# Paired maxima and exponents, and a new step table for the next batch's preparation, in a gated cross-attention and mixture-of-experts kernel

## The reference

```python
xn = layer_norm(ctx, gamma_x, beta_x)            # [8, 375, 256], the context
ln = layer_norm(layernorm(x), gamma_l, beta_l)   # [8, 112, 256], the latents
q = (ln @ Wq) * 64 ** -0.5                       # 8 heads of 64
k_x, v_x = split(xn @ Wkv); k_x = rope(k_x)      # 375 keys, rotated
k_l, v_l = split(ln @ Wkv)                       # 112 keys
attn = softmax(q @ concat(k_x, k_l).T)           # 112 x 487 for each head
x = x + tanh(g0) * (attn @ concat(v_x, v_l)) @ Wo
...
P = softmax(layernorm(x) @ Wg); P_norm = the two largest of P, normalized
x = x + tanh(g1) * sum_e P_norm[e] * (gelu(layernorm(x) @ W1[e] + b1[e]) @ W2[e] + b2[e])
```

## Time and profile before

| | |
|---|---|
| time, median of 3 runs | 532.35 us (531.82 to 533.09) |
| the profiled execution | 532.01 us, span 530.3 us |
| TensorE busy | 442.8 us, 84% of the span |
| VectorE busy | 303.9 us, 57% |
| ScalarE busy | 268.4 us, 51% |
| GpSimd busy | 192.1 us, 36% |
| mean granted TensorE clock | 0.919 of full speed |
| scores of batch 0 to scores of batch 7 | 72.75 to 283.47 us |

### The profile page before, as it was taken

How to read it: one execution, slowest core, us unless ns; L and a number is a source line. 1 busy time by engine, 2 the same in 40 slices (tenths; PEclk the granted TensorE clock), 3 DMA queues, 4 the chain that set the end, 5 groups by cost and what they waited for, 6 DMA issues and landing times. The chain is left out here.

```text
span 530.3 us, 9193 instructions
## 1 busy us (share of the span) xinstructions
PE 442.8 (84%) x3173; PEld 372.4 (70%) x3173; DVE 303.9 (57%) x715; ACT 268.4 (51%) x568; POOL 192.1 (36%) x211
## 2 busy tenths in 40 slices
PE   1689868897989979798888773589999999999990
PEld 1578646575756757575665662369999999999990
DVE  4564632436263453626354733548888888888850
ACT  2322245645646574564646611037676766776630
POOL 4231027272544627264460147301332222233322
PEclk9999969897999999799999965559999999999997
DMA  7200000000001009950008012576777778884323
GB/s 218 84 1 29 0 22 9 5 27 1 30 1 30 0 27 286 237 139 0 1 5 314 1 45 64 198 226 222 209 200 208 203 220 227 240 252 81 47 29 89
DMA packets 41863, 56.04 MB, mean 106 GB/s; under 512 B 1745, under 2 KB 37153, under 8 KB 41808
## 3 DMA queue, kind: packets, MB, share of 16 engines
q1 hardware_dynamic: 36864, 49.80, 30.8%
q0 software_dynamic: 4960, 5.72, 6.9%
HBM read 40.37 MB, written 16.07 MB: 106 GB/s over the span
## 5 line engine op out<-in xcount | busy, mean ns | idle before, releaser
L1356 POOL DMA_INDIRECT acc_scratch<-yv,xt x28 | 49.0, 1752 | 130.7 <-DVE yv L1509 126.5
L1378 ACT ACTIVATE hf<-ph,b1t 128x256 f32<-128x256 f32 x112 | 47.1, 472 | 48.3 <-PE ph L1584 47.7
L851 DVE TENSOR_REDUCE negmax<-sc 112x1 f32<-112x487 f32 x64 | 42.2, 660 | 37.2 <-PE sc L1092 37.2
L1092 PE MATMUL sc<-keys,queries 64*112 64x488 f32 x128 | 37.9, 671 | 24.0 <-ACT prob L649 22.3
L649 ACT ACTIVATE prob<-sc,negmax 112x487 f32<-112x487 f32 x64 | 43.0, 672 | 21.3 <-DVE negmax L851 21.3
L1117 PEld LDWEIGHTS po<-probt,vals 125*64 125x64 f32 (+1 forms) x512 | 27.5, 148 | 25.6 <-issue 16.3
L1100 PE MATMUL pt<-ident,prob 112*125 112x112 f32 x256 | 41.3, 286 | 3.4 <-ACT prob L649 3.4
L1100 PEld LDWEIGHTS pt<-ident,prob 112*125 112x125 f32 x256 | 37.0, 198 | 8.9 <-ACT prob L649 5.2
L1491 DVE TENSOR_TENSOR hl<-hf,hh 128x512 fp32r<-128x512 f32 x56 | 38.8, 693 | 1.9
L1489 DVE CAST hh<-hf 128x512 fp32r<-128x512 f32 x56 | 24.1, 431 | 23.8 <-ACT hf L1378 23.2
L657 ACT COPY probt<-pt 125x448 f32<-125x448 f32 x64 | 34.5, 540 | 5.0 <-PE pt L1100 4.9
(11 more groups left out here) (303 smaller groups left out, 1321.7 us busy)
## 6 DMA issues: line engine op xcount, KB each, us to landing
w_first<-in_L_ffn_W SPq DMA_DIRECT2D x10, 1024.0 KB, 8.4
w_next<-in_L_ffn_W SPq DMA_DIRECT2D x10, 1024.0 KB
rows_scratch<-blank SPq DMA_DIRECT2D x2, 4257.0 KB, 32.5
w_third<-in_L_ffn_W SPq DMA_DIRECT2D x8, 1024.0 KB, 8.0
xt<-rows_scratch SPq DMA_DIRECT2D x14, 258.0 KB, 2.8
ctx_t<-in_ctx SPq DMA_DIRECT2D x8, 375.0 KB
w_first<-in_L_xattn_Wkv SPq DMA_DIRECT2D x1, 1024.0 KB, 9.0
x_all<-in_x SPq DMA_DIRECT2D x2, 448.0 KB, 5.2
```

Of the source, the lines that this page charges most:

```text
L851: dve.tensor_reduce(negmax[:, h % 2:h % 2 + 1], sc[h % 2][0:M, 0:JA], AX, ALU.max, negate=True).then_inc(max_done.sem, 1)
L1092: pe.matmul(sc[u][0:M, 0:JP], queries[r, p, a], keys[r, p, a], start=True, stop=True, tile_position=(u * DH, 0)).then_inc(score_done.sem, 1)
L1356: pool.indirect_dma_start(out=acc_dram, out_offset=bass.IndirectOffsetOnAxis(ap=xt[i % 3][:, n, D + 1:D + 2].bitcast(I32), axis=0), in_=yv ...
L1378: last = act.activation(hf[:, n % 3, u], ph[n % 3][:, u * T:(u + 1) * T], ACT.Gelu, bias=b1t[:, col])
```

## The change

There are five parts.

1. Order in the pairs. VectorE does the maxima of heads h+2 and h+3 together in an even head h, and the two reciprocals (`invert`) together in an odd one. ScalarE does `keep_prob` first in a head, and both exponents, h+2 and h+3, in the even head h. Before, each head did one of each.
2. The table of steps. LEAD goes from 8 to 10, AHEAD (how many steps the second batch stands behind the first in the opening) from 13 to 15, and most steps have new numbers. SPLIT_AT is (2, 4, 6, 8) and OUTPUT_AT (9, 10, 12).
3. The copy of x1row into x_all goes from VectorE to POOL (`keep_x1`, behind the power of the output's norm), and the next x1row waits for it.
4. The opening: the low part of Wq is subtracted on VectorE, not POOL, the second norm of the latents stands ahead of the first split, and the latents' keys and values fall in other steps.
5. The second half of x is loaded ahead of the weights, and the four gamma and beta vectors by ScalarE's queue.

The core of the diff:

```diff
-        LEAD = 8
-        AHEAD = 13
+        LEAD = 10
+        AHEAD = 15
         VALUES_AT = (2, 4, 6, 8)
-        SPLIT_AT = (3, 4, 7, 8)
+        SPLIT_AT = (2, 4, 6, 8)
         PROJECT_AT = (9,)
-        OUTPUT_AT = (9, 10, 13)
+        OUTPUT_AT = (9, 10, 12)
...
# POOL, prepare
-                if s == 9:
+                if s == 10:
                     if not first:
                         rotate(pool, t, p, 0)
-                if s == 11:
+                if s == 13:
                     if not first:
                         rotate(pool, t, p, 1)
-                if s == 13:
+                if s == 16:
                     if not first:
                         rotate(pool, t, p, 2)
...
+            def keep_x1(t, p):
+                pool.wait_ge(x1_done.sem, x1_done.at(t, p, 1))
+                pool.tensor_copy(x_all[:, bass.ds(2 * t + p, 1), :].rearrange("q a d -> q (a d)"), x1row[:]) \
+                    .then_inc(x1_kept.sem, 1)
             def late_rstd(t, p, h, previous):
                 for n, batch in due(OUTPUT_AT[1:2], h, (t, p), previous):
                     output_rstd(*batch)
+                    keep_x1(*batch)
...
# ScalarE, head
+                keep_prob(t, p, h)
                 prepare_beside(prepare, h, 0, following, after)
-                keep_prob(t, p, h)
+                if h % 2 == 0:
+                    if h + 2 < H:
+                        exponent(t, p, h + 2)
+                        exponent(t, p, h + 3)
+                    elif following:
+                        exponent(*following, 0)
+                        exponent(*following, 1)
                 prepare_beside(prepare, h, 1, following, after)
                 late_high_out(t, p, h, previous)
-                if h + 2 < H:
-                    exponent(t, p, h + 2)
-                elif following:
-                    exponent(*following, h + 2 - H)
...
# VectorE, opening
+            latent_norm(1)
             split_latents(0)
-            latent_norm(1)
+            dve.wait_ge(whi_done, 1)
+            dve.tensor_tensor(deep[1][:, 0:4, :], w2s[:, 0:4, :], deep[0][:, 0:4, :].bitcast(F32),
+                              ALU.subtract).then_inc(wql_done, 1)
             split_latents(1)
...
# VectorE, output
+                    dve.wait_ge(x1_kept.sem, x1_kept.at(t, p, 0))
...
-                    dve.tensor_copy(x_all[:, row, :].rearrange("q a d -> q (a d)"), x1row[:])
...
# VectorE, head
-                if h + 1 < H:
-                    invert(t, p, h + 1)
-                elif following:
-                    invert(*following, 0)
+                if h % 2 == 0:
+                    if h + 2 < H:
+                        row_max(t, p, h + 2)
+                        row_max(t, p, h + 3)
+                    elif following:
+                        row_max(*following, 0)
+                        row_max(*following, 1)
                 prepare_beside(prepare, h, 0, following, after)
-                if h + 2 < H:
-                    row_max(t, p, h + 2)
-                elif following:
-                    row_max(*following, h + 2 - H)
                 prepare_beside(prepare, h, 1, following, after)
+                if h % 2:
+                    if h + 1 < H:
+                        invert(t, p, h + 1)
+                        invert(t, p, h + 2)
...
# TensorE, prepare: one line of the table
-                if s == 7:
+                if s == 8:
                     project_keys(t, p, 0)
```

More of the change, by code:

```diff
@@ L339, in frame @@
         def frame(eng, prepare, latents, begin, head, close):
-            for s in range(AHEAD + LEAD - 2):
+            for s in range(AHEAD + LEAD - 3):
                 prepare(0, 0, s, first=True)
@@ L345, in frame @@
             begin(0, 0)
-            for s in range(LEAD - 2, LEAD):
+            for s in range(LEAD - 3, LEAD):
                 prepare(0, 1, s)
@@ L387, in _ @@
             load_latents(0)
-            for n, v in enumerate((gamma_x, beta_x, gamma_l, beta_l)):
-                sp.dma_start(affine_rows[n * KD:(n + 1) * KD, :], v.rearrange("(k p) -> k p", p=P)) \
-                    .then_inc(affine_loaded, 16)
+            load_latents(1)
             sp.dma_start(w2s[:, 0:4, :].rearrange("p (k a) d -> p k (a d)", k=KD),
@@ L419, in _ @@
         def _(pool):
-            for c in (crstd_done, cl_done, rope_done, krow_done, orstd_done, row_copied):
+            for c in (crstd_done, cl_done, rope_done, krow_done, orstd_done, row_copied, x1_kept):
                 c.start(pool)
@@ L572, in latents @@
                     act.activation(gates[:], gates[:], ACT.Tanh).then_inc(tanh_done, 1)
+            for n, v in enumerate((gamma_x, beta_x, gamma_l, beta_l)):
+                act.dma_start(affine_rows[n * KD:(n + 1) * KD, :], v.rearrange("(k p) -> k p", p=P)) \
+                    .then_inc(affine_loaded, 16)
             act.wait_ge(wq_loaded, 16)
@@ L626, in prepare @@
                     split_context(t, p, 1)
-                if s == 8:
+                if s == 9:
                     raw_key(t, p, 0)
-                if s == 9:
+                if s == 11:
                     keep_value(t, p, 0)
-                if s == 10:
+                if s == 12:
                     raw_key(t, p, 1)
-                if s == 11:
+                if s == 14:
+                    keep_key(t, p, 0)
+                if s == 16:
+                    raw_key(t, p, 2)
+                if s == 17:
                     keep_value(t, p, 1)
-                if s == 12:
-                    raw_key(t, p, 2)
-                if s == 13:
-                    keep_key(t, p, 0)
+                if s == 19:
+                    keep_key(t, p, 1)
+                if s == 20:
                     keep_value(t, p, 2)
-                if s == 16:
-                    keep_key(t, p, 1)
-                if s == 18:
+                if s == 21:
                     keep_key(t, p, 2)
@@ L836, in prepare @@
                                           crstd[:, j:j + 1], ALU.subtract, ALU.mult).then_inc(cnorm_done.sem, 1)
-                if s == 9:
+                if s == 10:
                     if first:
                         rotate(dve, t, p, 0)
-                if s == 11:
+                if s == 12 and not first:
+                    copy_latents(t, p)
+                if s == 13:
                     if first:
                         rotate(dve, t, p, 1)
-                if s == 13:
+                if s == 16:
                     if first:
                         rotate(dve, t, p, 2)
-                if s == 14 and not first:
-                    copy_latents(t, p)
             def row_max(t, p, h):
@@ L865, in begin @@
                 invert(t, p, 0)
+                invert(t, p, 1)
             def output(t, p, part):
@@ L1065, in prepare @@
                     transpose_context(t, p, 1)
[L1066 removed]
+                if s == 8:
                     project_keys(t, p, 0)
[L1068 removed]
+                if s == 9:
                     project_values(t, p, 0)
[L1070 removed]
+                if s == 11:
                     project_keys(t, p, 1)
[L1072 removed]
+                if s == 13:
+                    transpose_keys(t, p, 0)
+                if s == 14:
+                    project_keys(t, p, 2)
+                if s == 15:
                     project_values(t, p, 1)
[L1074 to L1077 removed]
+                if s == 17:
+                    transpose_keys(t, p, 1)
+                if s == 18:
                     project_values(t, p, 2)
[L1079 to L1081 removed]
+                if s == 20:
                     transpose_keys(t, p, 2)
```

52 lines of the change are left out of this document (20 added, 32 removed).

## The result

The changed kernel takes 560.46 us (median of 4 runs, 557.13 to 561.60); the kernel before took 532.72 us on the same chip (4 runs, 531.82 to 535.26). The ratio is 1.050, 95% interval 1.044 to 1.056: slower by 5%, and outside the forecast range of 526 to 550. The profiled execution took 560.93 us, its span 559.2.

The account below looks back on a forecast made before the run. TensorE was taken as the bound (25.39 of 30.20 us busy). Five batches +13.3, opening -1.2, first batch -2.7, batch 6 +1.7, last stretch -1.5 sum to +9.6 on 532.01: 541.5 us, range 536 to 547, 8 of 10 526 to 550.

Parts of the forecast that it names:

- Stall 2.55: Each batch: TensorE's key transposes wait 2.55 us for POOL's third rotation, which starts behind the output norm's power and x1row copy.
- Stall 2.4: Each batch: the next context's transposes wait 2.4 us for VectorE's normalization, its small statistics operations held beside POOL's rotation.
- Stall 2.0: Each batch: the output projection waits 2.0 us for VectorE's heads, since out_t stands behind an exponent on ScalarE.
- Stall 1.2: Each batch: the next context's first projection waits 1.2 us for POOL's low part, behind ScalarE's exponent and five copies.
- I take the lost clock to stay hidden here: Five batches: no time added for TensorE's lower clock, since half-clock work behind the context's transposes runs into the next stall.
- rival B: TensorE's lost clock has a price, towards the upper end of the range; chance 0.15.
- From the last batch's scores on ... -1.5, bounds -5 and +2: Last batch's scores to the end: pairs save waits, the rotations' work is gone, ten POOL scatters stay; -1.5 us.
- it takes 25.1: First batch: 21.7 us of full-clock work, a key stall of 1.0 and a context stall of 2.4; -2.7 us against 27.86.
- Opening and batch 6: Opening and its end together -1.2 us, bounds -4 and +2; batch 6 30.4 us against 28.71, +1.7.
- About 0.2% (1.1 us) can be told from no change: Whole kernel: smallest time difference taken as distinguishable, about 0.2% or 1.1 us.
- A: Context's small statistics operations not held by POOL's rotation: 31.15 us a batch, 528.5 us in all, faster; chance 0.27.
- C: Stalls smaller than worked out, keys' and output projection's halved, small operations not held: 28.9 us a batch, 517 in all; chance 0.03.

Follow-up runs that it names:

- experiment 9: Changed kernel with the next context's statistics issued on VectorE in head 2 ahead of heads, no longer in head 3: 555.14 us, ratio 1.043.
- experiment 10: Changed kernel with 18 extra TensorE transposes ahead of the wait for the third rotated keys and 18 ahead of the next context's wait: 558.15 us, ratio 1.050.
- experiment 8: Changed kernel with 14 extra TensorE transposes of the identity ahead of the wait for the third rotated keys: 563.91 us, ratio 1.057.
- Experiment 3: Changed kernel with the router's second pick and placing ahead of heads on VectorE in the last batch: 554.49 us, ratio 1.042.
- experiment 1: Changed kernel with out_t issued between the two exponents of an even head, not behind the second: 514.99 us, ratio 0.966.
- experiment 7: Changed kernel with out_t between the two exponents and, in the last batch, the router's second pick and placing ahead of heads: 509.69 us, ratio 0.956.
- experiment 5: Kernel before with only the pairs (maxima, exponents, reciprocals; probabilities' copy first on ScalarE), keeping old table, opening and POOL: 550.50 us, ratio 1.034.
- experiment 6: Changed kernel without the pairs, one maximum, reciprocal and exponent a head, keeping the new table, opening and keep_x1: 557.76 us, ratio 1.048.
- experiment 2: Changed kernel with POOL's third rotation one step earlier, ahead of the power of the output's norm: 559.10 us, ratio 1.048.

## Why the prediction was wrong, and where it was right

**The four stalls, of which three came.** "Stall 2.55" at the keys: 2.3, with the transposes at T3 + 7.98 (forecast 8.2). "Stall 2.4" at the context: 2.4, at T3 + 11.06 (11.1). "Stall 2.0" at the projection: 1.8. "Stall 1.2" at the first projection of the context never came: no wait for the low part is in the list. So idle time is 6.6 us a batch (32.9 by 5) where the forecast had 8.15. The mechanism of the second stall was right at its root, the small operations held beside POOL's rotation (it was a sum and a square that were held, 2.40 and 1.23 us, and not the subtractions at 1.2 each), and experiment 9 took it away by that root. Its last link was another one: not the normalization, but the maxima behind the statistics, then the exponent and the copy of the keys behind it. It came out at the same time only because both paths end within some 0.7 us of each other (235.03 + 0.80 against 236.49).

**"I take the lost clock to stay hidden here."** This step failed: the term for TensorE's work in a batch was too small. The forecast set 25.4 us, from the one batch at full clock; the five batches before have 26.8 on average (134.01 by 5) at 0.94, and the changed ones 28.3 (141.35 by 5) at a mean clock of 0.88. So 28.3 + 6.6 = 34.9 against the forecast's 33.5. This is rival B, the price of the lost clock, to which the prediction gave 0.15 and the upper end of its range. That price was my estimate, and no run shows it by itself; the runs show 1.5 us more work a batch than before (28.3 against 26.8). Such a price adds to the forecast and doesn't stand beside it, and I gave the two separate chances as if one excluded the other. How much of the 2.9 us of stretched work lengthens a batch and how much only fills what would have been waiting is not settled: in the two traces experiment 10 gives 1.1 us a batch back, in the whole time nothing that can be told. In the traces of experiments 8 and 10 the clock goes with the gaps of this place: with the gap of 2.5 us left they took 1.97 us at a granted clock of 0.50, with both gaps filled 1.08 at 1.00.

**"From the last batch's scores on ... -1.5, bounds -5 and +2."** This is the step that failed most, by 10.97 us, and it is by itself more than half of the miss. I had worked it from what goes (waits of the scores, the rotations' work) and did not follow what stands behind heads on VectorE in that batch. The order shown ahead of the prediction was of two places in the loop; the last batch has a third one, in which VectorE issues the router's steps behind heads. The same rule by which I found the stalls (what is queued behind a waiting instruction, and who waits for that) finds it: pick_second behind the heads of head 4, place behind those of head 6, and ten scatters, one every 1.25 us, on POOL behind place. Experiment 3 gave 5.7 us of it back. The upper bound of +2 came from no row; the two waits of heads ahead of the router's steps, as the changed kernel's trace has them, are 1.90 and 3.75 us, and -1.5 + 5.65 is +4.2, already outside it. It is not out_t behind the exponent alone: with out_t moved the stretch up to the slots is 3.0 us shorter, with the router's steps moved 5.7, with both 8.2 (experiments 1, 3 and 7). The last 1.8 stay open.

**First batch, "it takes 25.1".** It took 27.10. The waits were right, 3.5 us idle against the 3.4 of the forecast; the work was not, 23.57 us busy against 21.7. The clock was 0.88 again, as before, and I had taken work at full clock as a base (where 24.01 x 0.88 would even be 21.1) while the gaps were still there.

**Opening and batch 6.** Both numbers are near, and neither shows that its working was right. The opening gave -1.65 us against -1.2, but by traces of one execution each, and with the same opening the first scores of the experiments stand anywhere from 69.8 to 71.7 us; experiment 5, which has the opening of before, has them at 71.4 and not at 72.75. So what the opening's parts are worth is not shown. Batch 6 took 30.43 us against 30.4 by luck: 26.14 of work and 4.3 idle, where the forecast had 24.4 and 5.75.

**"About 0.2% (1.1 us) can be told from no change."** The intervals of the ratios here are 0.4 to 0.8% to either side, 2 us or more, so a difference of 1.1 us cannot be told.

**The rivals.** A needed the small operations not to be held; they were held 2.40 and 1.23 us. In experiment 1, where heads comes early, they slip in ahead of the rotation, which is A's condition, and the kernel is faster than before. C's 517, which I gave 0.03 since "nothing in the order speaks for that", is about where the kernel stands with out_t one place earlier. That the number is near C's is luck: C had halved stalls in the changed order, and the order of experiment 1 is another. The forecast named each link of the chain as a wait written in the code; it did not say that the three stalls all hang on one instruction's place.

**Paired maxima and exponents.** That the scores' waits would go was right: one is left, of 0.5 us.

## What to carry to other kernels

Before an instruction that waits is moved up in an in-order queue, list what stood between its old place and the new one, and ask of each who waits for it; here a 0.25 us copy behind a 3 us wait cost 45 us over the kernel. Do this in every stretch in which the engine has other work behind the same instruction, the last iteration above all, since the steady loop does not show it. When a forecast adds idle time to a TensorE-bound stage, the slower work belongs into the sum and not beside it: here 28.3 us of work a batch, at a mean clock of 0.88, where 25.4 were set. And a change of several parts that is slower as a whole, and in each of its two main parts alone, can still be one edit away from being faster than the kernel before: judge the waits, not the sum.

## What the runs showed of the hardware that I had not expected

A small VectorE operation was held over two operations of POOL in a row, not one. In the changed kernel csum of 125x3 (229.63) began 0.13 us after the rotation's first multiply (229.50) and ended 2.40 us later, with the second (230.75 to 232.01). It took 2.40 to 2.46 us in five of six batches there and 2.38 to 2.39 in experiment 6, against 0.16 to 0.17 in the kernel before, where no rotation ran beside it. In the earlier trace rows the longest was 1.25. Between the second operation and the third two more small ones passed (231.96 and 232.03, 0.15 us each), and the square csq, begun 0.05 us after the third, was held for 1.23. Beside a rotation, two maxima took 1.24 us (experiment 1, 200.02), as in the earlier trace rows, and three bn_stats 1.08 (experiment 2, 228.56), as in the earlier trace rows.

The granted clock of TensorE fell to 0.50 where the forecast did not expect it, and the same gaps did not always have the same effect. In four batches of the kernel before, a gap of 0.48 us and one of 2.0 to 2.2 stand ahead of the same scores. These took 1.08 us at 156.57 and 186.96, at a clock of 1.00, and 1.97 at 124.89 and 217.13, at 0.50:

```profile
124.89 1.97 PE L1092 MATMUL sc<-keys,queries 64*112 64x488 f32 x4 [2.24 <-ACT prob L649]
```

So the one light stretch of the earlier trace rows, at full clock, was not enough to price the clock from. In experiment 1 gaps of 0.7 and 0.9 to 1.0 us stand ahead of a batch's first scores; these took 1.08 at 124.15 (clock 1.00) and 1.85 at 151.92 (0.57). In experiment 9 gaps of 2.31 and 0.96 us, with only four transposes between them, were followed by scores of 1.97 at a clock of 0.50:

```profile
193.56 0.65 PE L1077 MATMUL pk<-ident,krow 125*128 125x125 f32 x4 [2.31 <-POOL krow L380]
...
195.16 1.09 PE L1050 MATMUL tp<-ident,ctx_t 125*128 125x125 f32 x4 [0.96 <-DVE ctx_t L846]
...
197.00 1.97 PE L1113 MATMUL sc<-keys,queries 64*112 64x488 f32 x4
```
